# One layer of a graph network with mixing and expert weights on one core: tables, bounds, bias buffers and weighing moved between engines, constant products added on TensorE

## What is computed

```python
x = x + gnn(xn, W, a, src, dst) + mix(xn, w_ql, w_qr, w_key, w_value)
x = x + ffn(layernorm(x), gate_W, gate_b, expert_W, expert_b)
```

```python
scores = max((x @ gate_W + gate_b) / TEMP, EPS)
p = softmax(scores); topk_idx = top_k(p, 2)
w = max(p, W_THRES); w = w / (sum of w over the two chosen)
y = einsum('bsd,edf->bsef', x, expert_W) + expert_b
out = einsum('bsef,bse->bsf', y, comb) / 2        # comb = w where chosen, else 0
```

## Time and profile before

| | |
|---|---|
| three timed runs | 1250.13, 1252.03, 1251.67 us; median 1251.67 |
| the profiled execution | 1250.8 us, its span 1249.0 us |
| mean granted TensorE clock | 0.977 |
| busy: PE, DVE, ACT, POOL | 1182.7 (95%), 734.5 (59%), 325.5 (26%), 456.7 (37%) us |
| chain that ended last, by engine | PE 83%, DVE 6%, POOL 6%, DMA 2%, issue 2%, ACT 1% |
| `e_raw` transfers | 64 of 512 KB, 8.4 us from issue to landing in the median |

### The profile page before, as it was taken

One profiled execution on the slowest core, in us unless ns is written; L12 is line 12 of the kernel. 1 busy time (PEld: TensorE's weight loads), 2 busy tenths in 40 slices (PEclk: granted clock), 3 DMA queues, 4 the chain that ended last, 5 costly groups with the idle time before them and its releaser, 6 DMA issues.

```text
span 1249.0 us, 16313 instructions
## 1 busy us (share of the span) xinstructions
PE 1182.7 (95%) x5799; PEld 992.4 (79%) x5799; DVE 734.5 (59%) x1483; ACT 325.5 (26%) x438; POOL 456.7 (37%) x447
## 2 busy tenths in 40 slices
PE   6999999999999999999999999999946999999996
PEld 5788888878788889889977878888845788777874
DVE  7979522454334677777677447997475722543434
ACT  2411212232111111111012213333242521533333
POOL 3960677878685000000000006324126344334343
PEclk9999999999999999999999999999967999999998
DMA  5101442843321322212045651253256955785855
GB/s 206 35 34 34 119 120 69 272 130 86 92 52 29 88 89 89 93 60 61 23 138 182 202 155 49 105 199 111 98 195 193 365 117 86 204 263 93 242 89 131
DMA packets 91031, 156.08 MB, mean 125 GB/s; under 512 B 14786, under 2 KB 45244, under 8 KB 90836
## 3 DMA queue, kind: packets, MB, share of 16 engines
q1 hardware_dynamic: 75556, 129.76, 30.8%
q0 software_dynamic: 15408, 25.44, 11.7%
HBM read 112.95 MB, written 42.04 MB: 124 GB/s over the span
## 4 chain that ended last, share of the span: by engine, by line
PE 83%; DVE 6%; POOL 6%; DMA 2%; issue 2%; ACT 1%; DVEq 0%; ACTq 0%; POOLq 0%; SPq 0%
PE ps L1583 25%; PE ps L1584 25%; PE ps L1585 25%; POOL in L668 4%; DVE e_lo L1427 2%; PE ps L1711 2%; PE ps L1754 2%; PE ps L1823 1%; PE ps L1670 1%; DMA e_raw<-in_L_ffn_expert_W 1%; DMA q_in<-in_L_mix_w_query_right 1%; PE ps L1623 1%; ACT e_hi L949 1%; POOL pad_c L759 1%; POOL pad_r L758 1%
## 5 line engine op out<-in xcount | busy, mean ns | idle before, releaser
L683 POOL DMA_INDIRECT tab_d<-val_i,addr_i x160 | 206.0, 1287 | 109.5 <-issue 109.5
L1583 PE MATMUL ps<-e_hi,lt_hi 128*128 128x512 f32 x368 | 149.0, 405 | 7.9 <-DVE e_lo L1427 6.2
L698 POOL TENSOR_TENSOR att_part<-att 128x640 f32<-128x640 f32 x10 | 15.8, 1577 | 365.9 <-PE ps L1585 352.6
L1585 PE MATMUL ps<-e_hi,lt_lo 128*128 128x512 f32 x368 | 144.3, 392 | 0.0
L1584 PE MATMUL ps<-e_lo,lt_hi 128*128 128x512 f32 x368 | 144.1, 392 | 0.0
L1583 PE MATMUL ps<-xt_hi,q_hi 128*128 128x416 f32 (+1 forms) x384 | 142.9, 372 | 0.0
L1584 PE MATMUL ps<-xt_lo,q_hi 128*128 128x416 f32 (+1 forms) x384 | 136.1, 354 | 0.0
L1585 PE MATMUL ps<-xt_hi,q_lo 128*128 128x416 f32 (+1 forms) x384 | 135.5, 353 | 0.0
L1260 DVE TENSOR_TENSOR cnt<-ps,cnt 128x256 f32 x208 | 87.5, 421 | 40.7 <-PE ps L1711 25.5
L784 POOL DMA_INDIRECT out<-y,row_put x46 | 73.6, 1600 | 91.2 <-ACT y L991 72.6
L1583 PEld LDWEIGHTS ps<-e_hi,lt_hi 128*128 128x128 f32 x368 | 69.5, 189 | 30.9 <-DVE e_lo L1427 14.1
(11 more groups left out here) (288 smaller groups left out, 2673.6 us busy)
## 6 DMA issues: line engine op xcount, KB each, us to landing
e_raw<-in_L_ffn_expert_W SPq DMA_DIRECT2D x64, 512.0 KB, 8.4
acc<-in_x SPq DMA_DIRECT2D x18, 512.0 KB, 8.3
w_raw<-in_L_mix_w_key SPq DMA_DIRECT2D x16, 512.0 KB, 3.7
h_d<-hs SPq DMA_DIRECT2D x18, 256.0 KB, 2.0
q_in<-q_d SPq DMA_DIRECT2D x9, 512.0 KB, 5.2
xm<-in_x SPq DMA_DIRECT2D x18, 256.0 KB
h_in<-h_d SPq DMA_DIRECT2D x9, 512.0 KB, 5.8
mix_d<-xm SPq DMA_DIRECT2D x18, 256.0 KB
```

The costliest lines, as they stand in the source:

```text
L683: nc.gpsimd.indirect_dma_start(out=tab_d, out_offset=bass.IndirectOffsetOnAxis(ap=addr_i[0:EP, j:j + 1], axis=0), in_=val_i[0:EP, j:j + 1] ...
L1583: nc.tensor.matmul(o, lh, rh, start=(k == 0), stop=False)
L1585: return nc.tensor.matmul(o, ll, rh, start=False, stop=(k == last_k))
```

## The change

- Pad tables: GpSimd's sixteen instructions go; VectorE writes `last_c`, `pad_r`, `pad_c` with one instruction each, behind `tok_w`, after a new wait for GpSimd's `pad_t`.
- TensorE's nine reads of the bounds: six stay in front of the token products, three go behind the pad totals. Behind each stand 1 to 3 products of constants (`ident`, `ones`, f32, 128x128) into a spare bank, 19 in all.
- First tile: 28 products of `ones` with itself in front of the first product.
- Weighing: the left half stays on ScalarE, now in front of `block_hi` right (in the last expert in front of both); the right half goes to VectorE behind `block_lo` right (in the last expert in front of it). `s_sum2` becomes `s_y[0]` and `s_y[1]`.
- Biases: four buffers; those of experts 2 and 3 are loaded behind `s_wslot`, that of `e+3` when the blocks before expert `e` are done.

```diff
-        bias = at("bias", EX + 4 * D, [P, 2, D])
+        NBIAS = 4
+        bias = [at(f"bias{b}", word, [P, D]) for b, word in enumerate((EX + 4 * D, EX + 5 * D, YB + D, RAW + 3 * NT * NE))]
...
+            sp.wait_ge(s_wslot, 1)
+            for e in range(2, NBIAS):
+                load_bias(e)
             for e in range(NE - 1):
-                if e >= 1:
+                if 1 <= e and e + NBIAS - 1 < NE:
 
                     sp.wait_ge(s_ye, first_block[e] * 2 + 2)
-                    load_bias(e + 1)
+                    load_bias(e + NBIAS - 1)
...
-            step(G.tensor_tensor(pad_t[:, :], pad_ok[:, :], tokv[:, 0:1].to_broadcast([P, NE]), ALU.mult))
-            for e in range(NE):
-                G.tensor_scalar(pad_r[:, e, :], io16[:, :], pad_at[:, e:e + 1], None, ALU.is_equal)
-                last = G.tensor_scalar(pad_c[:, e, :], io16[:, 0:NSLOT], last_b[:, e:e + 1], pad_t[:, e:e + 1], ALU.is_equal, ALU.mult)
-            last.then_inc(s_pad, 1)
+            G.tensor_tensor(pad_t[:, :], pad_ok[:, :], tokv[:, 0:1].to_broadcast([P, NE]), ALU.mult).then_inc(s_padt, 1)
...
-                    pool.wait_ge(s_sum2, i * 2 + (2 + h))
+                    pool.wait_ge(s_y[h], i + 2)
...
+                def left_weighed(i):
+
+                    act.wait_ge(s_sc[0], i * 16 + 16)
+                    act.wait_ge(s_ye, i * 2 + 3)
+                    act.sem_inc(s_passed, 1)
+                    nc.scalar.activation(y[:, 0:HALF], yb[:, 0:HALF], ACT.Copy, scale=w_slot[:, bass.ds(i, 1)]).then_inc(s_y[0], 1)
+
                 with act.Fori(first_block[e], first_block[e + 1]) as i:
+                    if e == NE - 1:
+                        left_weighed(i)
                     for h in range(NH):
-                        c = slice(h * HALF, (h + 1) * HALF)
                         act.wait_ge(s_mm, i * 3 + (2 + h))
                         block_hi(i + 1, h)
-                        act.wait_ge(s_sc[h], i * 16 + 16)
-                        act.wait_ge(s_ye, i * 2 + (3 + h))
-                        act.sem_inc(s_passed, 1)
-                        nc.scalar.activation(y[:, c], yb[:, c], ACT.Copy, scale=w_slot[:, bass.ds(i, 1)]).then_inc(s_sum2, 1)
+                        if h == 0 and e < NE - 1:
+                            left_weighed(i)
...
+            dve.wait_ge(s_padt, 1)
+            V.tensor_tensor(last_c[:, :, :], io16[:, 0:NSLOT].unsqueeze(1).to_broadcast([P, NE, NSLOT]),
+                            last_b[:, :].unsqueeze(2).to_broadcast([P, NE, NSLOT]), ALU.is_equal)
+            link(V.tensor_tensor(pad_r[:, :, :], io16[:, :].unsqueeze(1).to_broadcast([P, NE, P]),
+                                 pad_at[:, :].unsqueeze(2).to_broadcast([P, NE, P]), ALU.is_equal))
+            V.tensor_tensor(pad_c[:, :, :], last_c[:, :, :], pad_t[:, :].unsqueeze(2).to_broadcast([P, NE, NSLOT]), ALU.mult).then_inc(s_pad, 1)
...
+                def right_weighed(i):
+
+                    c = slice(HALF, D)
+                    dve.wait_ge(s_sc[1], i * 16 + 16)
+                    dve.wait_ge(s_ye, i * 2 + 4)
+                    V.tensor_scalar(y[:, c], yb[:, c], w_slot[:, bass.ds(i, 1)], None, ALU.mult).then_inc(s_y[1], 1)
+
...
-                        dve.wait_ge(s_sum2, i * 2 + (1 + h))
+                        dve.wait_ge(s_y[h], i + 1)
                         dve.wait_ge(s_mm, i * 3 + (1 + 2 * h))
-                        V.tensor_tensor(yb[:, c], ps[:, h, :], bias[:, e % 2, c], ALU.add).then_inc(s_ye, 1)
+                        V.tensor_tensor(yb[:, c], ps[:, h, :], bias[e % NBIAS][:, c], ALU.add).then_inc(s_ye, 1)
+                        if h == 1 and e == NE - 1:
+                            right_weighed(i)
                         block_lo(i + 1, h)
+                        if h == 1 and e < NE - 1:
+                            right_weighed(i)
...
+            pe.wait_ge(s_const, 1)
+            for _ in range(28):
+                nc.tensor.matmul(ps[:, 7, 0:P], ones[:, :], ones[:, :], start=True, stop=True)
...
+            def keep_busy(times):
+
+                for _ in range(times):
+                    nc.tensor.matmul(ps[:, SPARE, 0:P], ident[:, :], ones[:, :], start=True, stop=True)
+
             pe.wait_ge(s_bounds, 1)
-            first_block = [pe.value_load(bounds[0:1, e:e + 1], min_val=0, max_val=NBLK) for e in range(NE + 1)]
+            first_block = []
+            for e in range(6):
+                first_block.append(pe.value_load(bounds[0:1, e:e + 1], min_val=0, max_val=NBLK))
+                keep_busy(2 if e < 4 else 1)
...
+            for e in range(6, NE + 1):
+                first_block.append(pe.value_load(bounds[0:1, e:e + 1], min_val=0, max_val=NBLK))
+                keep_busy(3)
```

More of the change, by code:

```diff
@@ L246, in gps_layer @@
         yb = at("yb", YB, [P, D])
+        bias = [at(f"bias{b}", word, [P, D]) for b, word in enumerate((EX + 4 * D, EX + 5 * D, YB + D, RAW + 3 * NT * NE))]
+        assert YB + 2 * D <= G and RAW + 3 * NT * NE + D <= YB
         slot_f = gate("slot_f", [P, NSLOT])
@@ L287, in gps_layer @@
         w_slot = small("w_slot", [P, NSLOT])
+        last_c = at("last_c", EX + 3 * D, [P, NE, NSLOT], f16)
         tok_now = small("tok_now", [P, 1], i32)
@@ L430, in gps_layer @@
         s_wtab, s_wsum, s_wslot = sem("s_wtab"), sem("s_wsum"), sem("s_wslot")
-        s_bias = [sem(f"s_bias{i}") for i in range(2)]
+        s_bias = [sem(f"s_bias{b}") for b in range(NBIAS)]
         s_ehi, s_elo = sem("s_ehi"), sem("s_elo")
@@ L435, in gps_layer @@
         s_passed = sem("s_passed")
-        s_put, s_sum2, s_sc = sem("s_put"), sem("s_sum2"), [sem(f"s_sc{h}") for h in range(2)]
+        s_put, s_y, s_sc = sem("s_put"), [sem(f"s_y{h}") for h in range(2)], [sem(f"s_sc{h}") for h in range(2)]
         s_gpos, s_non, s_nonp, s_pre, s_padt, s_pad, s_padp, s_rows, s_step = (sem(n) for n in (
@@ L602, in load_bias @@
             def load_bias(e):
-                sp.dma_start(bias[:, e % 2, :], expert_b[e:e + 1, :].partition_broadcast(P)).then_inc(s_bias[e % 2], 16)
+                sp.dma_start(bias[e % NBIAS][:, :], expert_b[e:e + 1, :].partition_broadcast(P)).then_inc(s_bias[e % NBIAS], 16)
             def load_target(t):
@@ L1515, in _ @@
             dve.sem_inc(s_ye, 2)
-            dve.sem_inc(s_sum2, 1)
+            dve.sem_inc(s_y[0], 1)
+            dve.sem_inc(s_y[1], 1)
             def block_lo(i, g):
@@ L1557, in _ @@
                 first_block.append(dve.value_load(bounds[0:1, e + 1:e + 2], min_val=1, max_val=NBLK))
-                dve.wait_ge(s_bias[e % 2], 16 * (e // 2 + 1))
+                dve.wait_ge(s_bias[e % NBIAS], 16 * (e // NBIAS + 1))
+                def right_weighed(i):
[3 more added lines that the diff above has]
+                    V.tensor_scalar(y[:, c], yb[:, c], w_slot[:, bass.ds(i, 1)], None, ALU.mult).then_inc(s_y[1], 1)
                 with dve.Fori(first_block[e], first_block[e + 1]) as i:
@@ L1806, in _ @@
             nc.tensor.matmul(ps[:, 7, NE:2 * NE], ones[:, :], g_tot[:, :], start=True, stop=True).then_inc(s_gtotp, 1)
+            SPARE = gnn_sum(NT - 1) % NB
+            assert SPARE in (0, 1, 3)
+            pe.wait_ge(*released(gnn_sum(NT - 1)))
+            def keep_busy(times):
+                for _ in range(times):
+                    nc.tensor.matmul(ps[:, SPARE, 0:P], ident[:, :], ones[:, :], start=True, stop=True)
             pe.wait_ge(s_bounds, 1)
-            first_block = [pe.value_load(bounds[0:1, e:e + 1], min_val=0, max_val=NBLK) for e in range(NE + 1)]
+            first_block = []
+            for e in range(6):
+                first_block.append(pe.value_load(bounds[0:1, e:e + 1], min_val=0, max_val=NBLK))
+                keep_busy(2 if e < 4 else 1)
             for c in range(2):
```

## The result

The changed kernel took **1247.08 us** in the median of 18 runs (1239.99 to 1253.22); the kernel before, on the same chip, 1252.11 (18 runs, 1249.62 to 1257.21). The ratio is **0.9943, 95% interval 0.9928 to 0.9958**: 7 us faster by this ratio (5.0 by the two medians), where 13 were forecast; 0.9943 of the 1251.67 us shown ahead is 1244.5. The profiled execution took 1247.32, span 1245.5 (before: 1249.0).

The account below looks back on a forecast made before the run. TensorE's stalls were taken as time, chiefly 8.9 us for GpSimd's pad tables (the 11.3 us start gains nothing). 9.5 + 2.6 + 0.9 = 13.0 us off 1251.67 gave 1238.7 us, range 1234 to 1244, forecast at 60%.

Parts of the forecast that it names:

- The fill ahead of the first tile, 0: The 28 products before tile 0 gain nothing: at most 1.6 us saved, gone by tile 4 or 5.
- The pad tables, 10.0 us at the first block's half: With tables on VectorE, block 0's transposes for the next block start at 947.0 instead of 957.03, 10.0 us earlier.
- The 19 products, 1.3 of them: Products behind TensorE's reads of the bounds keep the clock up for block 0, worth 1.3 us of the 10.0.
- The doubt about the transposes: Transposes at 937 might not count as clock work and let it fall before block 0; sum then 1.3 smaller.
- The gain shrinks to about 9.5: Blocks 0 to 3: transfers bind, so block 3's transposes start about 9.5 us before 998.01, between 7.8 and 10.8.
- The worst case of 2.9: Six bias loads and rows ahead of expert 2's rows, 1.7 each from 953 on, delay the train by 2.9 us.
- the row at 988.84: Row 4 of expert 3, which block 3 waits for; 15.3 us and nine transfers behind expert 2's row 4.
- The weighing, 2.6: Weighing split over two engines shortens changes of expert by 0.64 us, four times: 2.6, ends 0 and 3.9.
- The one transfer-bound step, counted at nothing: One of five expert changes behind block 3 has its transfer-bound kind of stall, which takes the 0.64 us back.
- weighing collides with GpSimd: Rival, 5%: VectorE's weighing waits for a running put; three changes lose 0.3 rather than win 0.64; 1241.5 us.
- The tail, 0.9: Last weighing ends 0.4 us earlier and last put no longer has one just ahead; ends 0.4 and 1.3.
- transfers eat more: Rival, 17%: biases and rows in front cost 2.9 us or more, later expert changes give nothing; 1244 us.

Follow-up runs that it names:

- z4: The changed kernel without the 28 constant products ahead of the first tile; 1247.24 us (12 runs).
- z2: The changed kernel with five constant products in TensorE's wait at 57.9 us, but pad tables built by GpSimd as before; 1251.41 us (12 runs).
- z3: The changed kernel with five constant products in the wait at 57.9 us, without the 19 products behind the reads of the bounds; 1243.19 us (6 runs).
- y4: The kernel before plus only five constant products in TensorE's wait at 57.9 us; 1247.96 us (12 runs), ratio 0.9966 to the kernel before.
- x4: The changed kernel plus five constant products in TensorE's wait at 57.9 us; 1242.11 us (6 runs), ratio 0.9918 to the kernel before.
- y1: The changed kernel with two bias buffers in place of four, filled in the order of the kernel before; 1244.7 us (1 run).
- x2: The changed kernel with SyncE's nine reads of the bounds moved between rows 2 and 3 of expert 1; 1248.3 us (1 run).
- z1: The changed kernel with five constant products at 57.9 us and the weighing of both halves back on ScalarE; 1242.32 us (6 runs).
- w4: The changed kernel with five constant products at 57.9 us, SyncE's reads of the bounds early, and biases 2 to 7 not loaded; 1230.5 us (1 run).

## Why the prediction was partly wrong

- **The fill ahead of the first tile, 0: right** (z4). The 28 products ended at 9.49 us, and the first tile began at 11.34 (11.3 before), again with 0.43 us between its products.
- **The pad tables, 10.0 us at the first block's half: right.** 10.3 measured, and z2 shows that it is the tables.
- **The 19 products, 1.3 of them: wrong** in why. The clock was up during the last nine (935.95 to 938.2) and fell again in the 2.54 us wait for the gather, as the transposes of 1.97 us show; block 0 was fed by VectorE in any case (z3). The doubt about the transposes was beside the point, the wait ahead of them had done it. On the rule weighed there (the Trainium skill, "TensorE: Matmul & The Clock Gate", Part 4, that transposes don't count for the clock) the kernel before speaks against: from 82.64 to 89.5 us it has nothing but f32 transposes on TensorE, the granted clock is 0.50 from 83 to 86.2, and 1.00 from 86.4 on.
- **"The gain shrinks to about 9.5": the step that failed.** It was 3.9 in the profile and 5.9 between y4 and x4. I let the train of rows move with VectorE's splits by 10.7 and allowed 1.2, at worst 2.9, for six transfers ahead of it. It moved by 5.5: expert 3's fifth row came at 70.11 where it had come at 75.57. Its head, expert 1's rows 3 to 7, hangs on the splits of expert 0, which stand where they stood. The engines had slack behind it before (a share of 0.86, 276 GB/s), and the earlier start used this up (0.96, 335 GB/s): a megabyte more had to pass (without it, in y1, the row comes 2.0 earlier), and SyncE's nine reads left the engines half idle in the middle (with the reads early, in x2, 2.4 earlier). I had priced single transfers against the row at 988.84, not added up what the stage moves from its first row to its last. The worst case of 2.9 can't be retraced either: six transfers of 1.7 from 953 on end at 963.2, and the row was due at 973.54 - 10.7 = 962.8. The second part of the same step is the clock, which I had left out there: behind the wait of 3.20 us for `yb` the half took 7.16 us, not 5.57, and cost 1.6 more. With the clock at 1.00 in both (y4, x4), row and block 3 both gain 5.9.
- **The weighing, 2.6: right per step, wrong in sum.** The step's stall fell by 0.54 to 0.83, against 0.64. The one transfer-bound step, counted at nothing, took 3 to 6 us more than before in nine of eleven profiles (x4 against z1: 4). In the profile after it happened to lose 0.2, and 3.4 were won in all. The rival *weighing collides with GpSimd* shows in the two smallest gains, 0.57 and 0.54: VectorE's weighing there took 0.74 and 0.79 us instead of 0.48, beside a copy on GpSimd that took 1.42 and 1.44 instead of 0.76.
- **The tail, 0.9: wrong**, 0.08. The last weighing ends 0.2 earlier behind the last transposes, not 0.4, and the put's start 1.8 us behind the weighing is not caused by the put ahead of it, which now stands 5.4 us in front, not 3.8. What causes it stays open.
- **The measure.** The profile of before that I worked from had the full clock at 60 us; so its time lies at the better end of what the kernel does, and the changed kernel's own did not. This moved the two profiled times by 4 us against each other: 3.9 at block 3, 3.4 by the weighing and 0.1 in the tail are 7.4 us won in the stage, and 3.5 are left of them (1249.0 - 1245.5). The ratio, over 18 runs of each, says 7.

The rival *transfers eat more* (17%, 1244) is nearest to what happened, but its number is partly luck. Rows in front did cost more than 2.9: the row lost 5.2 of its 10.7. But it had the later steps give nothing, and they gave 3.4, and it had no place for the clock, which took 1.6.

## What to carry to other kernels

Before a stage is started earlier, look for what of it can't go earlier, and add up what its transfers move from there to the last row that it waits for. Divided by the rate that such a mix reaches (330 to 360 GB/s here) this is an estimate of how early its end can be; it is no exact bound, as x2 and w4 show. A broadcast of one row to all partitions is a full transfer in that sum. A queue that must do n late-fed items before an evacuation turns the last one's lateness into a stall of the whole pipeline.

A stall of TensorE can cost twice, once as the wait and once as the clock behind it; so compare stages by the moment of an arrival, and look at the granted clock before a difference in block times is put down to anything else. A wait ahead of a long run of products is worth looking at for the clock: a few constant products in the one at 57.9 us were worth 4 us in the kernel before and 3 to 5 in the changed one (by the ratios, by the medians).

## What the runs showed of the hardware

- A wait of 1.4 us with full work before and behind it was followed by 1.2 GHz for some 7 to 10 us in all seven profiles of changed kernels without products there, and by 2.4 GHz in the one of the kernel before; with 1.28 us of constant products in it, by 2.4 GHz in twelve of twelve.
- Ahead of block 3 waits of 0.9 to 2.1 us were followed by a granted clock of 1.00 in seven profiles, and waits of 2.5 to 8.3 us by 0.64 to 0.77 over the next 7.1 to 8.4 us in ten. So a wait of 1.4 us alone does not tell what the clock will do.
- The DMA engines at a share of 1.0 moved up to 420 GB/s of rows, but 323 to 347 over 4 us while puts with their additions and gathers ran among them.
- Nine reads of a register on SyncE take 5.2 us, in which its queue asks for nothing: half of the DMA engines' time from 952 to 956 went unused.
